# Delta-rule block with routed columns: routing ranks moved ahead of the second chunk's solve, on TensorE and on VectorE

## What is computed

```
# attention: gated delta rule, 16 heads of 32
q, k, v, gate, beta = projections of x;  alpha = exp(-exp(A_log) * softplus(x @ Wa.T + dt_bias))
q, k = normalised by their length per head
for each token: S = S * a;  delta = (v - k @ S) * beta;  S = S + outer(k, delta);  y = q @ S
out = (rmsnorm(y, norm_w) * silu(gate)) @ Wo.T + bo
# ffn: 16 columns of 128 neurons, the best one per token
logits = cosine(x, col_emb) + sigmoid(gelu(x @ gate_w1 + gate_b1) @ gate_w2 + gate_b2)
mask = one_hot(argmax(logits));  weights = mask * softmax(logits)
out = layernorm((gelu(x @ W_cols + b_cols) * weights) @ proj_w + proj_b + x) * ln_g + ln_b
```

## Time and profile before

| | |
|---|---|
| three runs, us | 3474.14, 3475.73, 3475.79 |
| profiled execution, us | 3470.64 |
| its span, us | 3468.3 |
| busy share: TensorE, VectorE, GpSimd, ScalarE | 83%, 74%, 55%, 48% |
| mean granted clock of TensorE | 0.909 of full speed |

### The profile page before, as it was taken

One profiled execution on the slowest core, in us unless ns is written; L12 is line 12 of the kernel. 1 busy time (PEld: TensorE's weight loads), 2 busy tenths in 40 slices (PEclk: granted clock), 3 DMA queues, 4 the chain that ended last, 5 costly groups with the idle time before them and its releaser, 6 DMA issues.

```text
span 3468.3 us, 125046 instructions
## 1 busy us (share of the span) xinstructions
PE 2887.7 (83%) x51176; PEld 2252.4 (65%) x51176; DVE 2583.5 (74%) x10710; ACT 1662.8 (48%) x4105; POOL 1913.3 (55%) x2903
## 2 busy tenths in 40 slices
PE   5898898989988888988889888898888888437774
PEld 4676676777777666767667676676767666324443
DVE  1667877777777777778877778777777778647986
ACT  3344544444455444444554444444544544236664
POOL 1555555555555555555566555555554555416887
PEclk9898999989999999999999999999989999658997
DMA  3554444444444444444444444444444444545763
GB/s 107 125 127 108 113 118 120 121 117 124 117 110 108 115 116 105 121 115 113 119 115 121 120 121 118 124 115 118 116 110 107 109 117 110 152 143 105 131 124 63
DMA packets 349964, 403.80 MB, mean 116 GB/s; under 512 B 31169, under 2 KB 293953, under 8 KB 348881
## 3 DMA queue, kind: packets, MB, share of 16 engines
q1 hardware_dynamic: 332752, 362.10, 41.6%
q0 software_dynamic: 16640, 33.71, 5.0%
HBM read 323.97 MB, written 75.93 MB: 115 GB/s over the span
## 4 chain that ended last, share of the span: by engine, by line
PE 53%; DVE 26%; ACT 11%; issue 4%; DMA 2%; POOL 1%; ACTq 1%; SPq 0%; DVEq 0%; POOLq 0%
PE work L435 23%; DVE kq L1156 6%; DVE u L1143 5%; DVE Ut L1140 5%; PE work L528 5%; PE work L536 3%; DVE stats L1103 3%; PE u L474 3%; PE work L444 2%; PE su L496 2%; PE u L677 2%; PE kkq L465 2%; PE work L504 2%; PE u L488 2%; DMA pairs<-pair_rows 1%
## 5 line engine op out<-in xcount | busy, mean ns | idle before, releaser
L435 PE MATMUL work<-xT,w_sb 128*128 128x256 f32 x5120 | 1327.8, 418 | 201.5 <-DVE rows L1217 151.6
L975 POOL TENSOR_TENSOR pairs<-pairs,beta 128x240 f32<-128x240 f32 (+14 forms) x1920 | 870.4, 489 | 936.8 <-DMA pairs<-pair_rows 936.7
L435 PEld LDWEIGHTS work<-xT,w_sb 128*128 128x128 f32 x5120 | 1061.6, 211 | 433.9 <-DVE rows L1217 163.2
L1143 DVE TENSOR_TENSOR u<-u,Ut 128x120 f32<-128x120 f32 (+14 forms) x3840 | 708.8, 226 | 0.0
L1140 DVE TENSOR_TENSOR Ut<-pairs,u 128x120 f32<-128x120 f32 (+14 forms) x3840 | 689.1, 216 | 3.7 <-POOL pairs L975 2.4
L1156 DVE TENSOR_TENSOR kq<-kq,qr 128x512 f32<-128x512 f32 x128 | 346.0, 2724 | 137.3 <-ACT qr L771 137.3
L1127 DVE TENSOR_TENSOR u<-vT,u 128x128 f32<-128x128 f32 x256 | 61.8, 287 | 320.2 <-PE u L474 292.3
L1008 POOL TENSOR_TENSOR xfw<-xfw,pb_sb 128x1024 f32<-128x1024 f32 x32 | 85.9, 2684 | 359.1 <-DVE slot L1220 359.1
L528 PE MATMUL work<-wo_sb,ctxT 128*128 128x512 f32 x512 | 241.6, 615 | 4.1 <-issue 4.1
L763 ACT ACTIVATE kq<-work 128x512 f32<-128x512 f32 x128 | 75.9, 593 | 263.0 <-PE work L435 262.9
L770 ACT ACTIVATE qr<-work 128x512 f32<-128x512 f32 x128 | 76.9, 600 | 247.9 <-PE work L444 247.9
(11 more groups left out here) (237 smaller groups left out, 5301.3 us busy)
## 6 DMA issues: line engine op xcount, KB each, us to landing
pairs<-pair_rows SPq DMA_DIRECT2D x512, 256.0 KB, 3.6
pairs<-pair_rows SPq DMA_DIRECT2D x512, 224.0 KB, 3.8
xt<-in_x SPq DMA_DIRECT2D x66, 256.0 KB, 4.5
pair_rows<-Ak SPq DMA_DIRECT2D x64, 256.0 KB, 2.5
x<-in_x SPq DMA_DIRECT2D x64, 256.0 KB, 4.6
out<-x SPq DMA_DIRECT2D x64, 256.0 KB, 3.3
wo_sb<-xs_rows SPq DMA_DIRECT2D x30, 258.0 KB, 3.0
w_sb<-in_w_in SPq DMA_DIRECT2D x1, 5120.0 KB, 14.7
```

Of the source, the lines that this page charges most:

```text
L435: mm = pe.matmul(w[:, half * BT:(half + 1) * BT], w_sb[:, f, j * D + hg * P:j * D + (hg + 1) * P], xT[:, f, :], start=(f == 0), stop=(f == ...
L975: ins = nc.gpsimd.tensor_tensor(a, a, beta[:, :, t:t + WID[t0]], ALU.mult)
L1143: link(v.tensor_tensor(uk[:, g, at + 1:at + 1 + n], uk[:, g, at + 1:at + 1 + n], Ut[:, g, 0:n], ALU.subtract), f"pairs_free{j}" if i and t ...
```

## The change

On TensorE `ranks` is issued ahead of `state_to_u(1)` instead of behind it. On VectorE `rows_of_tokens` is issued ahead of the wait for `uk_full` and `solve_half(1, 0)` instead of behind them. Nothing else differs: the same instructions, tiles, banks and semaphores.

```
                 if after:
                     output_projection(1)
-                if chain:
-                    state_to_u(1)
                 if late:
                     ranks()
+                if chain:
+                    state_to_u(1)
                 if ahead:
                     squares_sum(2)
...
                     output_rows(1)
                     token_stats(y, y_mv, 1, "y_mv_ready")
+                if late:
+                    rows_of_tokens()
                 if chain:
                     take(dve, "uk_full")
                     solve_half(1, 0)
-                if late:
-                    rows_of_tokens()
                 if ahead:
                     scale(1)
```

More of the change, by code:

```diff
@@ L610, in step @@
                     output_projection(1)
+                if late:
+                    ranks()
                 if chain:
                     state_to_u(1)
-                if late:
-                    ranks()
                 if ahead:
```

## The result

| | before | after |
|---|---|---|
| median of four runs, us | 3474.93 | 3199.66 |
| lowest and highest, us | 3465.81, 3475.79 | 3186.68, 3206.09 |
| profiled execution, us | 3470.64 | 3204.02 |
| its span, us | 3468.3 | 3201.6 |
| mean granted clock of TensorE | 0.909 | 0.938 |

The ratio is 0.9209, with a 95% interval of 0.9174 to 0.9244. The change takes 275 us off by the medians and 266.6 from one profiled execution to the other. The sum of the prediction was 242. One of the four runs, 3206.09, falls inside.

What follows compares the result with a forecast made beforehand. The step was taken as bound by GpSimd's run, released by `slot`, not by TensorE's stall. 17 x 8.8 + 12 x 7.8 = 243, corrected to 242 us; 3470.6 - 242 + 5.1 = 3234, say 3235; range 3205 to 3325.

Steps and rivals of the forecast that it cites:

- The sum of the prediction: Whole kernel: 17 steps gaining 8.8 us and 12 gaining 7.8, with small corrections, 242 us together.
- None of this is on the chain as such, since the scaling waits for GpSimd anyway.: TensorE at the gate projection: removing its 5.2 us stall and the slow stretch behind it gains nothing by itself.
- gets through only among the last, narrow multiplications of the run, whenever it arrives: VectorE's third late scaling of k, arriving at X+7.4 inside GpSimd's run: held 7.86 us, to X+15.26.
- Slot and GpSimd's idle time: GpSimd before L1008: `slot` ready 9.9 us earlier; 12 of 29 steps limited by idle time, mean 9.4, minus 0.6.
- What is given back: Behind GpSimd's run: three scalings meet it instead of one, so 1.0 us of each step's gain is lost.
- The rule on the port: VectorE and GpSimd's shared SBUF ports, held for one instruction: a waiting scaling gets in at most 1.3 us later.
- slow TensorE only at the first `v` projection: Expected sign in the profile after: TensorE's slow clock remains at that projection and nowhere else.
- sum's reserves of 0.35 a step: Allowances for GpSimd taking turns with scalings (half of 0.5 us) and for TensorE (8.9 cut to 8.8).
- The clock as a rival: TensorE's slow stretches cost 5 us: in half of the steps 3305 us, chance 0.14; in all 3380, chance 0.05.
- No gain: An unseen wait holds the scaling at its old place, only TensorE's stall goes: 3475 us; chance 0.05.
- slower: Row instructions and L1218's stand lie on the chain through the second chunk's solve: 3504 to 3554 us; chance 0.06.
- First boundary: Scalings get in at GpSimd's first instruction boundary, nothing given back, TensorE bounds at 8.8 us: 3216 us; chance 0.07.

Runs made afterwards that it cites:

- run 4: Kernel before with only L1215 and L1217, which free TensorE's bank, ahead of the solve; the three instructions that finish `slot` stay behind it; 3389.26 us.
- run 8: Kernel after with the first two late scalings put into the middle of the solve and the third reading its factor from PSUM; 3126.29 us.
- run 5: Kernel before in its old order, with the third late scaling reading its factor from PSUM instead of SBUF; 3373.98 us, ratio 0.9749.
- runs 3 and 5: Run 3: kernel after with L1217, which frees TensorE's bank, put back behind the solve, `slot` still early; 3365.64 us. Run 5 has its own line.
- runs 9 and 10: The filled kernels: two and three idle matmuls ahead of the `v` projection, in the kernel before (run 9, 3452.3 us) and after (run 10, 3202.79 us).
- tensor_alone: Kernel before with only TensorE's half, `ranks` ahead of `state_to_u(1)`; VectorE's row instructions stay behind the solve; 3470.12 us, ratio 1.0005.

## Why the prediction was right or wrong

**What bounds the step.** Right in its main point. The long wait on the half-idle GpSimd was the one that counts: TensorE's stall is gone in run 4 and in the kernel after alike; one gains 76 us, the other 275, and what differs is the early `slot`. Wrong in a second one: "None of this is on the chain as such, since the scaling waits for GpSimd anyway." Run 4 took only TensorE's stall away and gained 3 us per step. What is wrong here is the reading "gets through only among the last, narrow multiplications of the run, whenever it arrives". It holds for most arrivals inside the run. At X to X+3.2 the scaling gets in, in each of run 4's steps, and the earlier trace rows had hinted at it with an arrival at X+5.9, its 1.18 us and the 5.11 us wait for the adds. The prediction used that step as a rival for the behaviour, and did not ask what would bring the scaling there in every step. In the kernel after this costs the sum little, for the scalings then come to the run from X+9.7 on; the sum failed elsewhere (under *The size*).

**Slot and GpSimd's idle time.** Right. Per step, solve(0, 1) to the next X fell by 9.24; the sum had (17 x 9.9 + 12 x 8.8) / 29 = 9.4. GpSimd's idle time before L1008 is 1.34 or 1.35 in 12 of 29 steps and 0.55 or 0.10 in 15, where it came from `dec` late; the prediction had about 1. The mean idle time of the 12 late steps before is 9.3, not 9.4 as the prediction says, which makes 1 us in all.

**What is given back.** Right in size. The turn of `xfw` was to come 1.0 later after X, with 0.25 in reserve for a worse taking of turns and 0.1 for TensorE. It came 1.08 later. The scalings ended 0.9 later (predicted start + 16.2; 16.1 in most steps). The statistics were done 0.70 later, and TensorE took the rest of 0.38: both were predicted at X_before+12.5, and run 8 shows that neither has much slack without the other.

**The rule on the port.** A waiting scaling did not get in at GpSimd's next boundary: three took 5.94 us, across the end of the first lot, both adds and the start of the second. By the rule (the Trainium skill, "SBUF — State Buffer", section "Who interferes with whom") GpSimd holds the pair for one instruction; the short wait that follows from it shows in 2 of 29 steps of the kernel after (0.81 and 0.79 us for the first scaling), while the usual one is 5.0. What the section says of operands, that a VectorE instruction with two SBUF inputs is the one in conflict, run 5 bears out with 0.69 against 7.86 us.

**The size.** From profile to profile the gain is 266.7, and 24.7 are missing in the sum. The first X came 13.75 us earlier, of which 3.8 are already there at the end of `output_projection(1)`, ahead of the first moved instruction (298.70 and 294.93). That is the clock in one place, in which the two executions differ by chance, first before, then after:

```profile
262.00:280.00 18.00, 18.00 (x320) 16.04 (x320) 12.95 (x72) 7.06 (x23) 13.16 (x21) 0.72 0.61 143
```

```profile
262.00:280.00 18.00, 18.00 (x342) 15.80 (x341) 17.40 (x94) 9.28 (x27) 11.65 (x19) 1.00 0.55 129
```

The 28 periods gave 245.1, against about 225 in the sum, the last step 9.76 against 9, and the end lost 1.9, about 1 more than the sum has. (Some 1.5 us of rounding in the sum remain.) So the missing part is 0.7 us per step, and the table of milestones places it. The stretch from the turn of `xfw` to the end of the `v` projection is 1.08 us shorter (10.23 to 9.15), which the prediction did not have. This is the step of the sum that failed: it left that projection slow in every step ("slow TensorE only at the first `v` projection") and put any gain there at nothing, without a reason. It measured 1.08 us per step: 0.21 in the wait ahead of it and 0.87 in the projection (6.04 to 5.17), of which 6 of 28 now run in 3.6 to 3.7 us and the slow ones take 5.6 instead of 6.0. Against it stand 0.46 us in the next step's first half (about 0.3 in TensorE's clock and 0.17 in its idle times of no named cause), and 0.2 at the slot. Of the sum's reserves of 0.35 a step 0.27 was not paid. Together 1.08 + 0.27 - 0.46 - 0.20 = 0.69. These are places in two traces, not an experiment: runs 3 and 5 turned a shorter `v` stretch into time, runs 9 and 10 hardly did, so it isn't shown that this term made the difference in the time. The remaining 9 us of the 33 between 242 and 275 are the profiled executions' distance from their medians, 4.3 below before and 4.4 above after.

**The clock as a rival.** In part. Long stretches show in 6 of 28 steps instead of 3, three of the six like the one at 734 us; that is far from half of the steps, and the mean cost is 0.45 us per step, or 13 us. It isn't shown that the change caused them: tensor_alone, as fast as the kernel before, has 8 in its profiled execution (3486.76, one of its slowest). What the clock costs in the `v` projection (2.4 us a step in the kernel before) is real in that place, and of it 0.6 at most is won by the medians when it is removed, in the kernel after nothing.

**The range.** Its lower end lay 30 us under the forecast, drawn from the sum's own terms, and held no room for the spread of executions. In later comparisons single executions of the kernel before went from 3444 to 3489, so 20 us or more either way would have had to stand in it. The slowest of them had a mean granted clock of 0.906 and the fastest one of 0.916. The upper end, by contrast, had 90 us for one rival. The mistake is one-sided: an unknown clock was priced as a loss alone, while the change also gave TensorE steps in which it comes to the `v` projection with less idle time behind it.

**The other rivals.** *No gain* and *slower* are excluded by the ratio. The five row instructions and L1218 did not lie on the chain. *First boundary* is excluded by the 5.94 us, although its time, 3216, was the nearest of all to the measured one: the time alone would have pointed to the wrong mechanism.

**Left open.** Why TensorE's clock falls in some steps at the key products and not in others; what TensorE waits for in the idle times of up to 2.4 us for which the profile names no other engine; and how much of the period in the filled kernels is SyncE's order and how much the clock. An experiment with the token transfer ahead of the pair fetches was not tried.

## What to carry to other kernels

When an engine that is idle half of the time has the longest wait, look at what it does without a gap after that wait, and which other engine's instructions stand beside it: an in-order run released late can set the whole step. When two waits are released by the same late instruction, cost them together and apart, for each may hide the other (76 and 100 us apart, 275 with both). And give the range the spread of single executions and the clock in both directions.

## What the runs showed of the hardware

- A VectorE multiplication of 128x512 with both inputs in SBUF took 7.86 us (6.3 to 8.3 in 28 of 29 steps) beside a gapless run on GpSimd, 1.29 for two beside GpSimd's scatters, and 0.69 in all 32 steps with the second input in PSUM.
- GpSimd pays for it too: L1008 took 2.72 us with a scaling in its way and 2.36 without, the eight narrow multiplications 3.85 with three scalings and 2.93 with one.
- Sixteen matmuls of 128x256 took 3.6 to 3.7 us at 2.4 GHz and 5.2 to 6.8 in the kernel before, behind two waits of 1.2 and 1.6 us. Idle matmuls of 1.03 and 1.46 us in those waits made it 3.64 in 28 of 28 steps, twice. The time of the kernel fell by 0.5% in one case and not at all in the other.
- TensorE's granted clock also fell to 0.56 where the engine had hardly stood idle, in some steps and not in others with the same work: 16 multiplications that write 16 columns each took 3.60 instead of 1.96 us there.
- TensorE stood idle for up to 2.4 us in the middle of 128 small matmuls in some steps, with no other engine named as the cause.
